# A two-layer attention kernel on one core: loops written out with constant waits, and part of the second layer's vector work given to GpSimd

## The chip, the cores and the metric

The kernel runs on 1 core of one Trainium2 chip. The metric is the device time of one execution in microseconds (us). The core has five engines that run side by side and meet at semaphores: TensorE (PE in the profile, with PEld for its weight loads), VectorE (DVE), ScalarE (ACT), GpSimd (POOL), and SyncE (SP), which here only issues DMAs. Before the change three runs took 2165.38, 2171.02 and 2171.84 us, a median of 2171.02 us.

## The reference, cut to what matters

The input is x of 16 batches x 512 tokens x 128 features, float32. Two layers follow each other, and each adds an attention and a feed-forward part to its input:

```
xn = layernorm(x)
x  = x + attn0(xn) + ffn0(xn)       # 16 heads of 8; q, k through low-rank maps and an RMS norm;
                                    # causal; ffn0: sigmoid gate * (square(relu(.)) @ W_v)
xn = layernorm(x)
x  = x + attn1(xn) + ffn1(xn)       # attn1: softmax(q k^T * scale + bias(position)) v, @ w_proj + b_proj
                                    # ffn1: gelu(xn @ W1) @ W2, W1 and W2 composed once from 32 low-rank pairs
```

So the last line of the second layer sums four things for each token: the residual x, the projected attention, the feed-forward output and b_proj. This sum is one place that the change touches.

## The kernel before, in words

**Bodies and slots.** Each layer is a software pipeline over the 16 batches. One step of it is a "body" (class `Body`). Body n does the scores and the exponentials of batch n, and beside them the preparation for later batches (n+1, n+2) and the closing work of batch n-1. A body has 4 units u (4 heads each) of 16 slots, 64 slots in all. In a slot TensorE computes one 128x512 tile of transposed scores (`scores_t`, L584), which ScalarE exponentiates (L848), and one tile of scores for the row maxima (`scores_max`, L601), which VectorE reduces (L1079 in the first layer, L1084 in the second, there two tiles in one instruction). Four tiles of the second kind fit in PSUM, so TensorE can be at most some three tiles ahead of VectorE (`wait(pe, s["red_done"], ...)`); two tiles of the first kind fit, so it waits for ScalarE's exponential before last (`exp_done`). Every four slots come eight matmuls of probabilities times values (L569).

**The other work.** Everything else is hung on slots by two tables written by hand, `WORK_USES` (uses of the one PSUM bank `work`: the slot at which TensorE fills it, how much later it is taken out, and the batch offset) and `OTHER_WORK`. Each engine walks the slots in order and does what is due on it; each engine's queue runs in that order. In the second layer these matter here:
- `QT` (slot 39) and `KT` (slot 44): queries and keys of batch n+2 are split into three bf16 parts. ScalarE makes the first part, VectorE the remainder (`leave_rest`, L1050), ScalarE the second part (L835), VectorE the third (`third_part`, L1054, three slots after the work bank was taken out first). In the first layer the third part is made on GpSimd (L1126).
- `PR` (slot 30): the projection of batch n-1. VectorE adds the PSUM result and the residual `x_res` (L1038), then the feed-forward output `ffn` (L1041), then the bias `bproj` (L1043), all into `x_new`. These two later additions count up the semaphore `post`.
- `STORE` (slot 32): GpSimd waits for `post` and writes `x_new` with four indirect DMAs (L1139).
- GpSimd multiplies the probabilities next to the diagonal by `near_bias`, once every four slots (L1197), 16 times a body. In the first layer it masks instead (L1183).
- `H0` to `H3` (slots 3, 9, 15, 24): the hidden tiles of the feed-forward part, each with two VectorE instructions (L1060 one slot later, L1066 three slots later). Both read two tensors from SBUF. At the start of each unit VectorE also writes the maxima as two bf16 parts (L963, L965).
- SyncE loads `x_res` at slot 0 (after `post` of the batch before) and `x_tile`, moves the bf16 parts to DRAM and back into `stacks` (L433), and the maxima from `mT` (L448).

**Loops.** Bodies 0 and 1 of a layer are written out, then a loop runs 5 times over two bodies (2 to 11), and bodies from 12 on are written out again: `run_first_layer` (the loop is at L221) and `run_second_layer` (L240). Between the layers `run_both_layers` lets the last bodies of the first layer and the first of the second alternate. In the loop the wait values depend on the loop register, so an engine computes each in a register first (`Body.count`, L250, returns `self.i * (2 * per) + fixed`). `wait_apart` (L253 to L260) puts such a wait in an instruction of its own with an increment of `passed` behind it. All five engines jump back at the loop's end.

## Time and profile before

| | us |
|---|---|
| median of 3 runs | 2171.02 |
| profiled execution | 2168.74 |
| its span, first to last instruction | 2166.6 |
| TensorE busy, share of the span | 1775.1 (82%) |
| VectorE busy | 1610.4 (74%) |
| ScalarE busy | 1338.4 (62%) |
| GpSimd busy | 800.3 (37%) |

The first layer takes roughly the time up to 980 us, the change-over up to 1200 us, the second layer the rest. No engine is busy all the time, so the shares alone do not say what an edit is worth. Since body follows body, the distance from an instruction in one body to the same instruction in the next is the price of a body, and what an engine waits for inside one body tells what sets it. [...]

### The profile page before, as it was taken

To read this page: it belongs to the slowest core of one execution; us is meant where nothing else is said; L and a number is where in the kernel's file an instruction comes from. 1 tells how busy PE (TensorE), PEld (TensorE's weight loads), DVE (VectorE), ACT (ScalarE), POOL (GpSimd) and SP (SyncE) were. 2 spreads that over 40 slices of the span, in tenths; PEclk is the share of its full clock that TensorE was granted. 3 is DMA by queue.
4 is the path that set the end of the run, shared out by engine and by line. 5 is a ranking of instruction groups with operands and counts; after the bars stand their busy time and mean duration, and the time that the engine had idled before them with its cause. 6 is when DMAs were issued, how large, how long until landed. Compare 5 with 4: busy or idle time off the path is not lost.

```text
span 2166.6 us, 41630 instructions
## 1 busy us (share of the span) xinstructions
PE 1775.1 (82%) x12618; PEld 722.7 (33%) x12618; DVE 1610.4 (74%) x2911; ACT 1338.4 (62%) x2518; POOL 800.3 (37%) x824
## 2 busy tenths in 40 slices
PE   5888877778887888878678888888888888888885
PEld 2543333333333333333222332323323333323221
DVE  4367777766677667766378888888898888888881
ACT  1246666655666556655347677777677776777764
POOL 3114443433344334443213344334444344343343
PEclk9769899988999889987669999999999999999998
DMA  7222221221222222220421122221212221222200
GB/s 234 42 45 60 60 56 47 60 61 46 55 52 53 61 55 60 60 55 16 78 45 43 37 60 46 50 56 40 46 44 59 49 50 34 59 45 53 52 11 15
DMA packets 133134, 116.46 MB, mean 54 GB/s; under 512 B 16856, under 2 KB 125664, under 8 KB 132960
## 3 DMA queue, kind: packets, MB, share of 16 engines
q1 hardware_dynamic: 126272, 100.64, 20.1%
q0 software_dynamic: 4096, 8.40, 1.4%
q10 hardware_dynamic: 2592, 5.24, 0.7%
q8 instruction: 93, 1.52, 0.3%
q14 instruction: 81, 0.66, 0.1%
HBM read 79.63 MB, written 33.55 MB: 52 GB/s over the span
## 4 chain that ended last, share of the span: by engine, by line
PE 43%; DVE 21%; issue 16%; ACT 8%; POOL 5%; DMA 3%; SPq 2%; DVEq 1%; ACTq 0%; POOLq 0%
PE pv_acc L569 12%; PE scores_transposed L584 10%; DVE maxs L1084 8%; ACT probs L848 4%; PE work L697 3%; DVE maxs L1079 3%; PE scores_for_max L601 3%; PE work L647 3%; DMA stacks<-parts_scratch 2%; PE work L669 2%; POOL probs L1183 2%; PE work L706 2%; PE work L619 2%; SPq L433 1%; POOL x_between_layers L1139 1%
## 5 line engine op out<-in xcount | busy, mean ns | idle before, releaser
L848 ACT ACTIVATE probs<-scores_transposed 128x512 f32<-128x512 f32 x1664 | 948.0, 600 | 442.6 <-PE scores_transposed L584 437.4
L601 PE MATMUL scores_for_max<-stacks 60*128 60x512 bf16 (+3 forms) x2048 | 659.9, 363 | 102.9 <-DVE maxs L1084 49.4
L584 PE MATMUL scores_transposed<-stacks 62*128 62x512 bf16 (+3 forms) x2048 | 641.6, 360 | 101.7 <-ACT probs L848 86.6
L1084 DVE TENSOR_REDUCE maxs<-scores_for_max 128x2 f32<-128x1024 f32 x512 | 610.9, 1219 | 110.6 <-PE scores_for_max L601 109.3
L1079 DVE TENSOR_REDUCE maxs<-scores_for_max 128x1 f32<-128x512 f32 (+3 forms) x1024 | 446.3, 483 | 253.6 <-PE scores_for_max L606 252.4
L1197 POOL TENSOR_TENSOR probs<-probs,near_bias 128x512 f32<-128x512 f32 x256 | 336.1, 1315 | 638.5 <-ACT probs L848 638.1
L569 PE MATMUL pv_acc<-probs,vals 128*32 128x512 f32 (+3 forms) x4096 | 495.6, 558 | 74.5 <-POOL probs L1183 48.5
L584 PEld LDWEIGHTS scores_transposed<-stacks 62*128 62x128 bf16 x2048 | 162.0, 95 | 755.6 <-ACT probs L848 483.0
L1183 POOL TENSOR_SCALAR_AFFINE_SELECT probs<-probs 128x512 f32<-128x512 f32 x256 | 158.4, 638 | 309.2 <-ACT probs L848 309.1
L601 PEld LDWEIGHTS scores_for_max<-stacks 60*128 60x128 bf16 x2048 | 175.9, 95 | 150.2 <-DVE maxs L1084 78.8
L604 PE MATMUL scores_for_max<-causal_halves,ident_halves 64*128 64x128 bf16 x1024 | 224.6, 233 | 0.0
L606 PE MATMUL scores_for_max<-causal_halves,ident_halves 64*128 64x64 bf16 x1024 | 197.6, 199 | 0.0
L569 PEld LDWEIGHTS pv_acc<-probs,vals 128*32 128x32 f32 x4096 | 83.9, 111 | 210.8 <-issue 127.2
L606 PEld LDWEIGHTS scores_for_max<-causal_halves,ident_halves 64*128 64x128 bf16 x1024 | 107.0, 105 | 55.8 <-issue 15.1
L604 PEld LDWEIGHTS scores_for_max<-causal_halves,ident_halves 64*128 64x128 bf16 x1024 | 98.2, 100 | 0.5
L619 PE MATMUL work<-ident,accS 128*128 128x128 f32 x512 | 93.5, 310 | 5.6 <-ACT mT L763 2.5
L647 PE MATMUL work<-wcat,xnT 128*128 128x512 f32 x128 | 84.6, 747 | 2.6 <-ACT big L784 0.9
L784 ACT ACTIVATE big<-work 128x512 f32<-128x512 f32 x64 | 38.4, 600 | 77.8 <-PE work L647 77.8
L1148 POOL TENSOR_TENSOR rstd<-mv,minus_half 128x4 f32<-128x4 f32 x32 | 33.3, 1039 | 142.1 <-DVE mv L990 142.1
L855 ACT ACTIVATE accS<-pv_acc 128x512 f32<-128x512 f32 x128 | 78.0, 609 | 3.6 <-PE pv_acc L569 3.6
L669 PE MATMUL work<-xnT,w 128*128 128x512 f32 x128 | 76.8, 684 | 2.3 <-DVE att L977 0.8
L1139 POOL DMA_INDIRECT out_dram<-x_new,slots_now x64 | 62.7, 980 | 36.3 <-issue 14.8
(126 smaller groups left out, 1895.9 us busy)
## 6 DMA issues: line engine op xcount, KB each, us to landing
stacks<-parts_scratch SPq DMA_DIRECT2D x768, 64.0 KB
parts_scratch<-parts SPq DMA_DIRECT2D x64, 384.0 KB, 3.0
x_tile<-in_L_attn_x_dram SPq DMA_DIRECT2D x16, 256.0 KB, 2.8
probs<-in_fc_B_dram ACTq DMA_DIRECT2D x1, 4096.0 KB, 19.3
stage_a<-in_fc_A_T_dram SPq DMA_DIRECT2D x1, 4096.0 KB, 16.9
stacks<-mT SPq DMA_DIRECT2D x256, 4.0 KB
x_res<-in_L_attn_x_dram SPq DMA_DIRECT2D x16, 256.0 KB, 3.3
x_tile<-x_between_layers SPq DMA_DIRECT2D x16, 256.0 KB, 2.8
```

The costliest lines, as they stand in the source:

```text
L569: last = mm(acc[32 * j:32 * j + 32, q0:T], vals[:, B.parity(off), kt, G * pu + j, :], probs[:, row, column:column + width], start=(kt == 0 ...
L584: last = mm(st[:, number % 2, column:column + T - q0], ks[p][rows, h, P * kt:P * kt + P], qs[p][rows, h, q0:T], start=True, stop=True)
L601: last = mm(s1[:, i % 4, 0:k1], qs[p][rows, h, P * qt:P * qt + P], ks[p][rows, h, 0:k1], start=True, stop=(layer == 1))
L604: mm(s1[:, i % 4, P * qt:k1], ident_halves[half, 0, :], causal_halves[half, 0, :], start=False, stop=False)
L606: last = mm(s1[:, i % 4, P * qt + HALF:k1], ident_halves[half, 1, :], causal_halves[half, 1, HALF:P], start=False, stop=True)
L619: last = tr(work[:, P * qt:P * qt + P], accS[:, P * qt:P * qt + P], ident[:])
L647: mm(work[:], xnT[:, B.parity(2), 1 + P * t:1 + P * t + P], wcat[:].rearrange("p a n -> p (a n)"), start=True, stop=True).then_inc(full, 1)
L848: fn(probs[:, row, :], st[:, number % 2, :], ACT.Exp, scale=SCALE).then_inc(s["exp_done"], 1)
L1079: v.reduce_max(maxs[:, su % 2, column:column + 1], s1[:, m % 4, 0:P * (qt + 1)], AX_X).then_inc(s["red_done"], 1)
L1084: v.reduce_max(maxs[:, su % 2, :].rearrange("p (e x) -> p e x", e=E)[:, :, column], s1[:, m % 4 - 1:m % 4 + 1, :], AX_X).then_inc(s["red_d ...
L1183: g.affine_select(out=diag, in_=diag, compare_op=ALU.is_ge, fill=0.0, base=0, pattern=[[0, G], [1, P]], channel_multiplier=-1).then_inc(s[ ...
L1197: g.tensor_tensor(diag, diag, near_bias[:, kt, :].unsqueeze(1).broadcast_to([P, G, P]), ALU.mult).then_inc(s["emul_pool"], 1)
```

## The change

Four edits, for all of which the diff is short:
1. Both loops go. Bodies 2 to 11 of each layer are written out like the others, so every wait value is a constant and there is no jump inside a layer.
2. In the second layer GpSimd adds `ffn` and `bproj` to `x_res` at slot 22 (`BESIDE`, semaphore `beside_done`), before the projection. VectorE's addition at `PR` then gives the finished `x_new` in one instruction; `post` is used in the first layer only.
3. In the second layer, too, GpSimd makes the third bf16 parts.
4. Waits follow: the store waits until `PR` was taken out of PSUM, SyncE's load of `x_res` for the same of the body before, and ScalarE's write of `ffn` for `beside_done`.

```
-    1: {"LN": (4, 2), "NORM": (16, 2), "STORE": (32, -1)},
+    1: {"LN": (4, 2), "NORM": (16, 2), "BESIDE": (22, -1), "STORE": (32, -1)},
...
-    with eng.Fori(0, PAIRS) as i:
-        for n in (STEADY, STEADY + 1):
-            run(body(Body(0, n, i)))
-    for n in range(STEADY + 2 * PAIRS, LAST - 1):
+    for n in range(STEADY, LAST - 1):
         run(body(Body(0, n)))
...
                     if u == 0 and B.has(-1):
-                        wait_apart(sp, s["post"], B.count(2, 0, -1), passed)
+                        if layer == 0:
+                            wait(sp, s["post"], B.count(2, 0, -1))
+                        elif B.has(-2):
+                            sp.wait_ge(s["work_taken"], Body(1, B.number - 1).use("PR") + 1)
...
                             if B.has(-1):
-                                act.wait_ge(s["post"], B.count(2, 2, -1))
+                                act.wait_ge(s["beside_done"], B.count(2, 2, -1))
...
-                        if layer == 1 and B.out(name, slot, 3):
-                            third_part(side)
...
                             filled("PR")
-                            dve.wait_ge(s["res_loaded"], B.count(16, 16, -1))
+                            dve.wait_ge(s["beside_done"], B.count(2, 2, -1))
                             wait(dve, s["x_stored"], B.count(16 * NT, 0, -1))
                             v.tensor_tensor(x_new[:].rearrange("p t d -> p (t d)"), work[:],
                                             x_res[:].rearrange("p t d -> p (t d)"), ALU.add).then_inc(taken, 1)
-                            taken_out("PR")
-                            link(v.tensor_tensor(x_new[:], x_new[:], ffn[:, B.parity(-1)], ALU.add),
-                                 "post", 2, 1, -1)
-                            v.tensor_tensor(x_new[:], x_new[:], bproj[:].unsqueeze(1).broadcast_to([P, NT, D]),
-                                            ALU.add).then_inc(s["post"], 1)
...
-                    wait_apart(pool, s["post"], B.count(2, 2, -1), passed)
+                    if layer == 0:
+                        pool.wait_ge(s["post"], B.count(2, 2, -1))
+                    else:
+                        pool.wait_ge(s["work_taken"], B.use("PR") + 1)
...
+                    else:
+                        if B.due("BESIDE", slot):
+                            pool.wait_ge(s["res_loaded"], B.count(16, 16, -1))
+                            g.tensor_tensor(x_res[:], x_res[:], ffn[:, B.parity(-1)], ALU.add
+                                            ).then_inc(s["beside_done"], 1)
+                            pool.wait_ge(s["beside_done"], B.count(2, 1, -1))
+                            g.tensor_tensor(x_res[:], x_res[:], bproj[:].unsqueeze(1).broadcast_to([P, NT, D]),
+                                            ALU.add).then_inc(s["beside_done"], 1)
+                    for side, name in enumerate(("QT", "KT")):
+                        if B.out(name, slot, 3):
+                            third_part(side)
```

What moves is shown at three places of a written-out body of the second layer. First VectorE's queue at `PR` (slot 30), before; a row names the line, the operation, its tiles and in brackets the semaphores that it waits for (`s1_ready`: a tile of scores is there):

```order
L1084 TENSOR_REDUCE maxs<-scores_for_max 128x2 [waits s1_ready_1]
L1038 TENSOR_TENSOR x_new<-work,x_res 128x512 [waits x_stored_1,res_loaded_1,work_full_1]
L1041 TENSOR_TENSOR x_new<-x_new,ffn 128x512 [waits work_taken_1]
L1043 TENSOR_TENSOR x_new<-x_new,bproj 128x512 [waits post_1]
L1084 TENSOR_REDUCE maxs<-scores_for_max 128x2 [waits s1_ready_1]
L963 TENSOR_SCALAR msp<-maxs 128x16 [waits red_done_1]
```

The same place of the same engine's queue now:

```order
L1051 SCALAR_TENSOR_TENSOR big<-fc,fd 128x512 [waits tanh_done_1]
L1069 TENSOR_REDUCE maxs<-scores_for_max 128x2 [waits s1_ready_1]
L1033 TENSOR_TENSOR x_new<-work,x_res 128x512 [waits x_stored_1,beside_done_1,work_full_1]
L1069 TENSOR_REDUCE maxs<-scores_for_max 128x2 [waits s1_ready_1]
L960 TENSOR_SCALAR msp<-maxs 128x16 [waits red_done_1]
```

Two additions between two reductions are gone, and the one that is left waits for GpSimd (`beside_done_1`) in place of the DMA.

Second, VectorE's queue in unit 2, around the first third part, before:

```order
L1084 TENSOR_REDUCE maxs<-scores_for_max 128x2 [waits s1_ready_1] x2
L1050 TENSOR_TENSOR rest<-work,parts 128x512 [waits part0_done_1,work_full_1]
L1084 TENSOR_REDUCE maxs<-scores_for_max 128x2 [waits s1_ready_1]
L1054 TENSOR_TENSOR parts<-rest,parts 128x512 [waits part1_done_1]
L1084 TENSOR_REDUCE maxs<-scores_for_max 128x2 [waits s1_ready_1] x2
```

And the same unit on the same engine now:

```order
L974 TENSOR_TENSOR att<-work,rsum 128x4x32 [waits rec_1]
L1069 TENSOR_REDUCE maxs<-scores_for_max 128x2 [waits s1_ready_1] x2
L1040 TENSOR_TENSOR rest<-work,parts 128x512 [waits part0_done_1,work_full_1]
L1069 TENSOR_REDUCE maxs<-scores_for_max 128x2 [waits s1_ready_1] x3
L1040 TENSOR_TENSOR rest<-work,parts 128x512 [waits part0_done_1,work_full_1]
```

The third part has left the row of reductions.

Third, GpSimd's queue of one body, from `LN` on, before; `probs<-probs,near_bias` is the multiplication of every four slots:

```order
L1148 TENSOR_TENSOR rstd<-mv,minus_half 128x4 [waits ln_1]
L1197 TENSOR_TENSOR probs<-probs,near_bias 128x4x128 [waits exp_done_1] x7
L1134 TENSOR_TENSOR slots_now<-slots_now,a_batch 128x4 [waits x_stored_1]
L1139 DMA out_dram<-x_new,slots_now 8192x128 [waits post_1,slots_moved_1]
L1139 DMA out_dram<-x_new,slots_now 8192x128 x3
L1197 TENSOR_TENSOR probs<-probs,near_bias 128x4x128 [waits exp_done_1] x9
```

The same stretch of GpSimd's queue now:

```order
L1136 TENSOR_TENSOR rstd<-mv,minus_half 128x4 [waits ln_1]
L1193 TENSOR_TENSOR probs<-probs,near_bias 128x4x128 [waits exp_done_1] x4
L1160 TENSOR_TENSOR x_res<-x_res,ffn 128x512 [waits res_loaded_1]
L1163 TENSOR_TENSOR x_res<-x_res,bproj 128x512 [waits beside_done_1]
L1193 TENSOR_TENSOR probs<-probs,near_bias 128x4x128 [waits exp_done_1] x3
L1119 TENSOR_TENSOR slots_now<-slots_now,a_batch 128x4 [waits x_stored_1]
L1127 DMA out_dram<-x_new,slots_now 8192x128 [waits work_taken_1,slots_moved_1]
L1127 DMA out_dram<-x_new,slots_now 8192x128 x3
L1193 TENSOR_TENSOR probs<-probs,near_bias 128x4x128 [waits exp_done_1] x2
L1111 TENSOR_TENSOR parts<-rest,parts 128x512 [waits part1_done_1]
L1193 TENSOR_TENSOR probs<-probs,near_bias 128x4x128 [waits exp_done_1] x2
L1111 TENSOR_TENSOR parts<-rest,parts 128x512 [waits part1_done_1]
```

Four instructions have come into GpSimd's queue: two additions behind the multiplication of slot 20, and two third parts, the first behind the multiplication of slot 40, the second behind that of slot 48.

## Rows read from the trace of the kernel before

**Rows 1.** Windows of the first layer: four bodies with a jump back; five without

```profile
core 0: us, PE busy (x) PEld busy (x) DVE busy (x) ACT busy (x) POOL busy (x), PEclk, DMA share, GB/s
...
sum 244.20, PE 195.57 PEld 90.54 DVE 170.61 ACT 142.44 POOL 93.02; mean PE 48.89 PEld 22.64 DVE 42.65 ACT 35.61 POOL 23.25
...
sum 287.94, PE 232.21 PEld 109.24 DVE 213.70 ACT 178.42 POOL 116.10; mean PE 46.44 PEld 21.85 DVE 42.74 ACT 35.68 POOL 23.22
```

**Rows 2.** Windows of the first layer: two bodies before the loop's steady part, two behind it

```profile
159.49:275.62 116.13, 96.85 (x886) 44.90 (x882) 83.50 (x208) 72.02 (x132) 46.39 (x57) 0.89 0.25 56
...
807.76:920.45 112.69, 92.88 (x869) 43.20 (x868) 84.83 (x209) 71.19 (x131) 46.53 (x58) 0.92 0.25 58
```

**Rows 3.** TensorE's queue at the jumps back: the first layer's, then the second's

```profile
L221 PEldq COMPARE_BRANCH  x5: 76/3717/4063, 351.1 to 826.4; - x5
L240 PEldq COMPARE_BRANCH  x5: 76/208/240, 1366.9 to 1895.5; - x5
```

**Rows 4.** Timeline, TensorE behind a jump, then the same place without one

```profile
355.31 1.35 PE L569 MATMUL pv_acc<-probs,vals 128*32 128x512 f32 x8 [3.81 <-issue]
...
412.20 1.07 PE L569 MATMUL pv_acc<-probs,vals 128*32 128x512 f32 x8 [0.79 <-ACT accS L855]
```

**Rows 5.** Instruction queues (packets, MB, share): first layer's loop; all that the second's has

```profile
q8 instruction: 44, 0.72, 0.6%
...
q14 instruction: 20, 0.16, 0.1%
```

**Rows 6.** Windows of the second layer: nine bodies of the loop, two mostly written out

```profile
1266.72:1861.69 594.97, 521.99 (x3098) 186.38 (x3096) 515.84 (x685) 429.39 (x828) 235.93 (x198) 0.98 0.21 49
1861.69:1992.70 131.01, 112.83 (x690) 38.44 (x688) 113.09 (x153) 95.27 (x184) 52.39 (x44) 0.99 0.20 49
```

**Rows 7.** Waits in eight bodies of the second layer's loop, 1266.72:1795.37 (us in total, times, longest)

```profile
PE scores_transposed L584 <- ACT probs L848: 31.0, 74, 1.0
PE scores_for_max L601 <- DVE maxs L1084: 25.7, 26, 1.9
```

**Rows 8.** Third part by shape in those eight bodies; bias addition by source (min/median/max ns)

```profile
L1054 DVE TENSOR_TENSOR parts<-rest,parts 128x512 bf16<-128x512 f32 x16 | 26.9, 1679 | 0.7
...
L1043 DVE TENSOR_TENSOR x_new<-x_new,bproj x16: 691/1643/1647, 1202.1 to 2154.5; 128x512 f32<-128x512 f32 x16
```

**Rows 9.** Timeline of one loop body: VectorE, GpSimd and TensorE at both moved places

```profile
1399.90 0.69 DVE L1041 TENSOR_TENSOR x_new<-x_new,ffn 128x512 f32<-128x512 f32 x1
1400.62 1.64 DVE L1043 TENSOR_TENSOR x_new<-x_new,bproj 128x512 f32<-128x512 f32 x1
...
1399.99 1.73 POOL L1197 TENSOR_TENSOR probs<-probs,near_bias 128x512 f32<-128x512 f32 x1 [2.45 <-ACT probs L848]
...
1403.46 0.39 PE L601 MATMUL scores_for_max<-stacks 60*128 60x512 bf16 x1 [1.23 <-DVE maxs L1084]
...
1411.85 3.62 DVE L1054 TENSOR_TENSOR parts<-rest,parts 128x512 bf16<-128x512 f32 x1
...
1412.41 2.50 POOL L1197 TENSOR_TENSOR probs<-probs,near_bias 128x512 f32<-128x512 f32 x2
...
1416.67 0.47 PE L601 MATMUL scores_for_max<-stacks 60*128 60x512 bf16 x2 [1.93 <-DVE maxs L1084]
```

**Rows 10.** Windows of two loop bodies: with the 3.62 us row, without it

```profile
1399.17:1465.43 66.26, 57.80 (x346) 20.64 (x344) 57.96 (x77) 47.81 (x92) 26.19 (x22) 0.97 0.21 48
...
1531.31:1597.22 65.91, 58.75 (x346) 20.95 (x344) 55.87 (x77) 47.61 (x92) 26.23 (x22) 0.97 0.20 48
```

**Rows 11.** GpSimd's instructions of the kinds added: third part, addition (min/median/max ns)

```profile
L1126 POOL TENSOR_TENSOR parts<-rest,parts x32: 1152/1153/2471, 48.2 to 936.5; 128x512 bf16<-128x512 f32 x32
...
L1157 POOL TENSOR_TENSOR x_new<-x_res,att x16: 1268/1274/1297, 199.0 to 1062.6; 128x512 f32<-128x512 f32 x16
```

**Rows 12.** Timeline, slots 20 and 30 of one loop body, GpSimd and VectorE

```profile
1457.85 1.27 POOL L1197 TENSOR_TENSOR probs<-probs,near_bias 128x512 f32<-128x512 f32 x1 [1.38 <-ACT probs L848]
...
1465.43 0.69 DVE L1038 TENSOR_TENSOR x_new<-work,x_res 128x512 f32<-128x512 f32 x1
```

More of the change, by code:

```diff
@@ L239, in run_second_layer @@
         run(body(Body(1, n)))
-    with eng.Fori(0, PAIRS) as i:
-        for n in (STEADY, STEADY + 1):
-            run(body(Body(1, n, i)))
-    for n in range(STEADY + 2 * PAIRS, LAST + 1):
+    for n in range(STEADY, LAST + 1):
         run(body(Body(1, n)))
@@ L371, in build @@
                 "red_done", "msplit", "ln", "xn_done", "mix_done", "rms", "rest_done",
-                "rec", "gelu", "hidden_done",
+                "beside_done", "rec", "gelu", "hidden_done",
                 "part2_done", "post",
@@ L1050, in leave_rest @@
                     v.tensor_tensor(rest[:, side], work[:], parts[:, side, 0, :], ALU.subtract).then_inc(taken, 1)
-                def third_part(side):
-                    dve.wait_ge(s["part1_done"], B.count(2, side + 1, 2))
-                    v.tensor_tensor(parts[:, side, 2, :], rest[:, side], parts[:, side, 1, :],
-                                    ALU.subtract).then_inc(s["part2_done"], 1)
                 def gelu_inner(f):
@@ L1168, in other @@
                             g.tensor_tensor(k, k, big[:, :, 2 * P:3 * P], ALU.add).then_inc(s["k_done"], 1)
-                        for side, name in enumerate(("QT", "KT")):
-                            if B.out(name, slot, 3):
-                                third_part(side)
+                    else:
[9 more added lines that the diff above has]
+                            third_part(side)
                 def mask(off, u, kt):
```

## The prediction

> **What bounds the kernel now.** I read the distances from body to body first, since the pipeline repeats, then what TensorE and VectorE wait for inside a body, then the timeline at the places that the change touches.
>
> In the first layer a body is measured from one reciprocal of the RMS norm (slot 34) to the next. Nine such distances lie within the loop. The four that hold the jump back sum to 244.20 us, 61.05 each; the five without it to 287.94 us, 57.59 each [rows 1]. Written-out bodies before and behind take 116.13 and 112.69 us for two, 57.2 each on average [rows 2]. So the jump costs 3.5 us. Its cause stands in TensorE's queue: the branch takes 3717 ns at the median, and only the last one, which falls through, 76 ns [rows 3]. Behind the jump at 351.1 TensorE lies idle for 3.81 us, where in a body without one it waits 0.79 us at the same instruction [rows 4]. In this loop the queue that loads TensorE's instructions moved 44 packets; in the second layer's loop it does not appear at all, the answer lists only the other engines' 20 [rows 5], and the jump there takes 208 ns at the median [rows 3]. The first loop's pair of bodies is loaded anew each time, the second's is not.
>
> [...]
>
> In the second layer nine loop bodies take 594.97 us, 66.1 each, and the next two distances, mostly written out, 131.01 us, 65.5 each [rows 6]. In a body of 66.1 us TensorE is busy 58.0 us and VectorE 57.3 us (521.99/9 and 515.84/9): both are close to full, and they wait for each other. Over eight bodies TensorE waits 25.7 us for VectorE's reductions, 3.2 a body, and 31.0 us for ScalarE's exponentials, 3.9 a body [rows 7]. Two places make most of the first sum [rows 9]. At the projection VectorE does three additions between two reductions, the last of 1.64 us, and TensorE is idle 1.23 us until the next reduction has freed a tile. In unit 2 the third part takes 3.62 us, while GpSimd runs two multiplications back to back, and TensorE is idle 1.93 us. The same kinds of instruction take 0.69 us when nothing is beside them (691 ns is the least for the bias addition) [rows 8]: the rest is waiting for GpSimd.
>
> **The change part by part.**
>
> *First loop written out.* The jumps: 4 x 3.46 us (61.05 less 57.59) = 13.8 us. From below, 4 x 3.02 us (3.81 less 0.79, rows 4) = 12.1 us. The rest of the loop's cost, register arithmetic in front of each wait: 57.59 less 57.2 = 0.4 a body, 10 bodies, 4 us. It lies between 0 and 12 us, because the last two written-out bodies take 56.35 and the first two 58.07 [rows 2]. I take 18 us for the layer, bounds 10 and 26. What is late next at the old jump is ScalarE's copy of the accumulator, the 0.79 us already subtracted.
>
> *Second loop written out.* 66.1 less 65.5 = 0.6 us a body; I take 0.5 for ten bodies, as part of it can overlap the next term: 5 us, bounds 0 and 8. TensorE must now load its instructions here as well; the written-out bodies in the 65.5 us do so already.
>
> *VectorE's two additions at `PR`.* Removed: 0.69 + 1.64 = 2.3 us of VectorE a body [rows 9]. TensorE was idle 1.23 us behind them, so at most about that much is gained at once; I take 1.2.
>
> *The third parts.* Removed from VectorE: 2 x 1.68 us a body on average (1679 ns, rows 8). TensorE was idle 1.93 us in a body with the 3.62 us row. But bodies without it are not shorter by that: 65.91 against 66.26 us at the same mean clock, 0.97 [rows 10]. A mean of 0.97 means that each had its low-level stretch, and in the second the third part fell behind GpSimd's two multiplications in time. I read this as TensorE being late there for another reason, the low clock behind the stall at `PR`, which hid the difference. With both stalls gone neither delay should remain. I take 1.8 us a body for unit 2 and its clock, which with the 1.2 makes 3.0.
>
> Together 3.0 a body is a little under the 3.2 that TensorE waits for VectorE [rows 7]. Lower bound 1.0: both stalls go and TensorE meets ScalarE's exponentials earlier in place of VectorE. Upper bound 4.3: TensorE's own work and its waits for ScalarE, 58.0 + 3.9 = 61.9 us, leave no more of the 66.1. It holds in the 14 bodies that have all this work: 42 us, bounds 14 and 60. In the last body the two additions stand on the path: 0.69 + 0.69 = 1.4 us.
>
> *GpSimd's side.* Third parts cost it 1.15 us each, additions 1.27 [rows 11]: 4.9 us a body on top of 26.2 busy of 66.1 [rows 6], so 31 us, and it is idle half the time. The order on its queue decides. Slot 22: the multiplication of slot 20 ends at 1459.1, two additions end at about 1461.7, the projection's addition starts at 1465.43 [rows 12], so `beside_done` is 3.7 us early. (The addition with the broadcast bias has no row on GpSimd; between 1.15 and 2.5 us, its fastest and slowest two-input rows of this size, I take 1.27.) Behind these additions wait the multiplications of slots 24 and later, whose probabilities TensorE wants a unit (some 16 us) later. Third parts: GpSimd reaches them behind a multiplication that waits for the exponential of slot 43 or 51, so ScalarE's second part (slots 41 and 47) is always there; the DMA that takes the parts stands on SyncE's queue behind a wait for slot 54. `x_res` is loaded at slot 0, and needed at 22 in place of 30. None of this costs anything as long as GpSimd does not fall some ten slots behind.
>
> *Contention.* The rows that were held are gone from VectorE. But VectorE keeps eight gelu instructions and four bf16 splits of the maxima a body with two SBUF inputs, and GpSimd has four more instructions to meet them. The additions of slot 22 run up to VectorE's slot 25 with H3's first gelu instruction. A meeting costs between nothing and the 2.9 us of the 3.62 us row; two short ones a body are in my 3.0.
>
> [...]
>
> **The sum.** 18 + 5 + 42 + 1.4 = 66 us. The profiled execution took 2168.74 us (span 2166.6 and 2.1 around), which gives 2102 us. The median of the runs is 2171.02, 2.3 more; against it the forecast is 2104 us.
>
> **The rivals.**
> 1. *The second layer hardly moves.* TensorE takes up the freed time in waits for ScalarE or in the low clock, and gains 1.0 a body: 18 + 5 + 14 + 1.4 = 38 us, 2133 us. For it: rows 10, where 2.9 us less on VectorE gave 0.35 us. Against: that body still had the other stall.
> 2. *TensorE's own work becomes the bound.* All waits for VectorE go, 4.3 a body, and the first layer gives its upper 26: 26 + 8 + 60 + 1.4 = 95 us, 2076 us. For it: VectorE falls to about 51.6 us of work (57.3 less 5.7) against TensorE's 58. Against: VectorE's load is uneven, and unit 1 alone has H3, the normalisation and `PR`.
> 3. *Slower: loading instructions stalls TensorE in the second layer.* Its loop loads nothing now. A body of it has 346 + 344 matmuls and weight loads [rows 10], one of the first layer some 884 (886 + 882 for two, rows 2), and nine of those moved 44 packets: that is 3.8 packets a body, 38 for ten. If each stalled TensorE like a jump, 3.0 us, that is 114 us; less the 66 gained, 2219 us. It decides from 1.7 us a packet (66/38). Against it: the bodies behind each loop already run so and are the faster ones [rows 2, 6]. The same price would come from GpSimd holding VectorE three times a body.
> 4. *The change does not do what it says.* The last addition waits for GpSimd where it waited for a DMA; were `beside_done` late, the stall at `PR` would stay. It needs GpSimd 3.7 us later than read, and takes the 1.2 a body away, 17 us: 2121 us.
>
> **How the numbers follow.** Forecast, 2090 to 2120: 0.58. Rival 1: 0.17. Rival 2: 0.16. Rival 3: 0.04. Rival 4: 0.05. The likeliest time is 2104 us. The range reaches into both neighbours, 2072 to 2138. Within 0.3% (6.5 us, about what a measurement of this kernel can tell from no change) is left only by a partial rival 3: 0.03; slower 0.04; faster 0.93.
>
> **What the changed profile would show.** No branch rows in TensorE's queue and no idle time over 1.5 us in front of L569 at the places of the jumps; about 57 us a body in the first layer. In the second, bodies of 62.6 us (66.1 less 3.5); TensorE's waits for reductions down from 3.2 to below 1 us a body, its waits for exponentials about as before; VectorE near 51.6 us a body; the third parts on GpSimd at 1.15 us; a low clock less often in unit 2. The queue q8 appears in the second layer. I am wrong if bodies of the second layer stay above 65 us, if the gelu rows (L1060, L1066) grow to several us beside GpSimd, or if idle time by "issue" stands in front of TensorE's instructions every few us.

## The result and the profile after

The changed kernel takes 2084.22 us (median of 4 runs, 2083.3 to 2087.44), the kernel before 2169.42 us beside it. The ratio is 0.9612, with a 95% interval of 0.9592 to 0.9631. So it is 85 us faster where I had forecast 66 us (2104 us). The time lies in the whole range of 2072 to 2138 us, but outside the forecast's own 2090 to 2120, on the side of rival 2 (2076 us). The profiled execution took 2087.44 us with a span of 2085.7 us.

First, part 1 of the page of the changed kernel (busy time, share of the span, instructions):

```profile
PE 1712.9 (82%) x12618; PEld 692.7 (33%) x12618; DVE 1541.2 (74%) x2847; ACT 1333.7 (64%) x2518; POOL 870.5 (42%) x888
```

VectorE has 64 instructions fewer and GpSimd 64 more, four a batch, as the diff says.

Next, windows of before: the ten loop bodies of the first layer, and twelve bodies of the second from the first `x_new` addition on. The columns are those of rows 1; PEclk is TensorE's granted clock as a share of full speed. The clock records behind it hold two values in these traces, 1 and 0.5, here called full and half clock.

```profile
275.62:864.02 588.40, 474.59 (x4341) 221.64 (x4340) 425.94 (x1040) 356.43 (x651) 232.38 (x290) 0.91 0.23 56
1200.66:1992.70 792.04, 693.06 (x4130) 245.04 (x4128) 684.18 (x913) 572.33 (x1105) 314.34 (x263) 0.98 0.21 49
```

The same two stretches of the changed kernel:

```profile
275.88:836.59 560.71, 455.99 (x4341) 212.84 (x4341) 429.13 (x1040) 355.75 (x651) 233.17 (x290) 0.95 0.24 58
1173.75:1923.05 749.30, 658.45 (x4130) 223.79 (x4128) 623.11 (x865) 568.80 (x1105) 365.77 (x311) 1.00 0.22 52
```

The first stretch gives 27.7 us (I had 18, and 26 as the upper bound), the second 42.7. Up to the first stretch nothing changes (275.6 and 275.9), and between the two neither (336.6 and 337.2). The rest, from 1992.70 and 1923.05 to the end of the span, falls from 173.9 to 162.7, 11.2 us. That adds up to the 80.9 us between the spans. A body of the second layer takes 62.4 us (749.30/12), where I had 62.6 and rows 6 show 66.1 and 65.5. TensorE's mean clock over the twelve bodies is 1.00, with no record of half clock, where before it is 0.98, with nine stretches of 3.4 us at 0.5. How far can one profiled execution be trusted? The twelve bodies take 749.0 to 749.4 us in all eight traces that share this code of the second layer. The ten bodies of the first layer are not so steady: a second trace of the changed kernel (further down) has 568.80 us in place of 560.71. Over more traces the gain holds: three with this loop take 592.1 us on average, six without it 563.7.

TensorE's waits in eight bodies of the second layer, 1236.17:1735.80, which answer to rows 7 (us in total, times, longest):

```profile
PE scores_transposed L581 <- ACT probs L845: 37.2, 98, 0.6
...
PE scores_for_max L598 <- DVE maxs L1069: 3.5, 8, 0.5
```

The wait for VectorE's reductions went from 25.7 to 3.5 us, that for the exponentials only from 31.0 to 37.2. So the freed time was not eaten by ScalarE, and rival 1 is out. Rival 2 came half true: nearly all of the wait for VectorE went, and the first layer went past its bound, but a body of the second layer got 3.7 us shorter and not 5.1 (the rival's 4.3 and 0.8). At the projection one addition now stands between two reductions, and GpSimd's third part begins without hindering VectorE (timeline of the changed kernel, first VectorE, then GpSimd; compare rows 9):

```profile
1298.59 0.68 DVE L1033 TENSOR_TENSOR x_new<-work,x_res 128x512 f32<-128x512 f32 x1
1299.19 1.21 DVE L1069 TENSOR_REDUCE maxs<-scores_for_max 128x2 f32<-128x1024 f32 x1
...
1309.99 2.51 POOL L1193 TENSOR_TENSOR probs<-probs,near_bias 128x512 f32<-128x512 f32 x2
1312.44 1.16 POOL L1111 TENSOR_TENSOR parts<-rest,parts 128x512 bf16<-128x512 f32 x1
```

The bias addition, which had no row on GpSimd, by its source line (min/median/max ns); then the instruction queues in the same eight bodies:

```profile
L1163 POOL TENSOR_TENSOR x_res<-x_res,bproj x16: 1273/1281/1289, 1168.8 to 2067.4; 128x512 f32<-128x512 f32 x16
```

```profile
q8 instruction: 22, 0.36, 0.3%
q14 instruction: 20, 0.16, 0.1%
```

The addition with a broadcast input takes 1281 ns at the median, the plain one 1274 [rows 11]. The queue q8, absent from the old loop [rows 5], now moves 22 packets, 2.8 a body (I had 3.8). The twelve bodies all take 62.4 to 62.6 us, so no stall shows at them.

### The profile page after: what moved, and what is told of

The parts are those of the page before. It is cut to its first block, busy times and chain, and to the rows that moved or that the text cites. A ratio compares the mean times of both kernels' runs of the same rounds, so it can differ in the third digit from the quotient of the medians.

```text
span 2085.7 us, 34983 instructions
## 1 busy us (share of the span) xinstructions
PE 1712.9 (82%) x12618; PEld 692.7 (33%) x12618; DVE 1541.2 (74%) x2847; ACT 1333.7 (64%) x2518; POOL 870.5 (42%) x888
## 4 chain that ended last, share of the span: by engine, by line
PE 45%; DVE 23%; ACT 14%; issue 9%; DMA 4%; SPq 3%; POOL 2%; DVEq 0%; POOLq 0%; ACTq 0%
PE pv_acc L566 12%; PE scores_transposed L581 10%; ACT probs L845 7%; DVE maxs L1069 6%; DVE maxs L1064 5%; DMA stacks<-parts_scratch 4%; PE work L694 4%; PE scores_for_max L598 3%; PE work L644 2%; SPq L427 2%; PE work L666 2%; DVE xn L991 2%; PE work L703 2%; DVE msp L962 1%; PE work L616 1%
## 5 line engine op out<-in xcount | busy, mean ns | idle before, releaser
L581 PE MATMUL scores_transposed<-stacks 62*128 62x512 bf16 (+3 forms) x2048 | 631.8, 354 | 122.1 <-ACT probs L845 97.3
L598 PE MATMUL scores_for_max<-stacks 60*128 60x512 bf16 (+3 forms) x2048 | 651.8, 359 | 72.3 <-DVE maxs L1064 33.6
L1193 POOL TENSOR_TENSOR probs<-probs,near_bias 128x512 f32<-128x512 f32 x256 | 329.7, 1291 | 511.3 <-ACT probs L845 510.9
L566 PE MATMUL pv_acc<-probs,vals 128*32 128x512 f32 (+3 forms) x4096 | 480.0, 542 | 61.9 <-issue 33.9
L603 PEld LDWEIGHTS scores_for_max<-causal_halves,ident_halves 64*128 64x128 bf16 x1024 | 105.4, 103 | 54.8 <-issue 12.1
L1111 POOL TENSOR_TENSOR parts<-rest,parts 128x512 bf16<-128x512 f32 x64 | 75.3, 1177 | 96.8 <-ACT parts L832 96.8
L616 PE MATMUL work<-ident,accS 128*128 128x128 f32 x512 | 86.1, 292 | 6.3 <-ACT mT L760 3.3
```

Of the source, the lines that this page charges most:

```text
L566: last = mm(acc[32 * j:32 * j + 32, q0:T], vals[:, B.parity(off), kt, G * pu + j, :], probs[:, row, column:column + width], start=(kt == 0 ...
L581: last = mm(st[:, number % 2, column:column + T - q0], ks[p][rows, h, P * kt:P * kt + P], qs[p][rows, h, q0:T], start=True, stop=True)
L598: last = mm(s1[:, i % 4, 0:k1], qs[p][rows, h, P * qt:P * qt + P], ks[p][rows, h, 0:k1], start=True, stop=(layer == 1))
L603: last = mm(s1[:, i % 4, P * qt + HALF:k1], ident_halves[half, 1, :], causal_halves[half, 1, HALF:P], start=False, stop=True)
L1193: g.tensor_tensor(diag, diag, near_bias[:, kt, :].unsqueeze(1).broadcast_to([P, G, P]), ALU.mult).then_inc(s["emul_pool"], 1)
```

## The experiments

All were compared with the kernel before on the same chip. The chips differ by some microseconds, so I compare ratios, and the windows of the profiles.

**Loops written out, nothing moved.** The kernel before with only this edit, in both layers:

```
-    with eng.Fori(0, PAIRS) as i:
-        for n in (STEADY, STEADY + 1):
-            run(body(Body(1, n, i)))
-    for n in range(STEADY + 2 * PAIRS, LAST + 1):
+    for n in range(STEADY, LAST + 1):
```

> Both loops written out, nothing moved to GpSimd. Theory (the gains add up, the first layer gave 27.7 us and not my 18): 28 us from the first layer and 5 from the second, about 2136 us against 2169, ratio 0.985. Rival (the first layer's extra 10 us over my 18 came with the moves or with a lucky clock): 23 us, about 2146 us, ratio 0.989. The second layer's bodies at 65.5 us by both.

Measured: 2135.35 us, ratio 0.9842 (0.9785 to 0.9899). Windows of the two stretches:

```profile
275.77:837.91 562.14, 463.75 (x4341) 216.69 (x4341) 422.34 (x1040) 355.73 (x651) 233.26 (x290) 0.93 0.24 58
1177.72:1957.05 779.33, 667.53 (x4130) 224.81 (x4128) 682.71 (x914) 572.67 (x1105) 313.74 (x263) 1.00 0.21 50
```

The first layer's gain is all here: 26.3 us of the 27.7. The second layer surprised: 12.7 us, where I had 5. Its bodies take 64.9 us on average (779.33/12), not the 65.5 of the bodies behind the old loop. The total came out as expected.

**Moves only.** The changed kernel with both loops back.

> Both loops kept, the sum and the third parts on GpSimd. Theory (gains add up): 52.5 us less 5 for the second loop, 47 us, about 2122 us, ratio 0.978; bodies of the second layer near 62.9 us, first layer as before at 58.8. Rival (the moves need constant waits to pay, since register arithmetic stands in TensorE's and VectorE's queues): 35 us or less, bodies of 63.7 us or more, ratio above 0.984.

Measured: 2120.57 us, ratio 0.9772 (0.9716 to 0.9828).

```profile
273.87:869.45 595.58, 481.28 (x4341) 225.06 (x4340) 426.73 (x1041) 356.94 (x651) 232.20 (x290) 0.90 0.24 55
1202.86:1957.41 754.55, 677.14 (x4130) 243.98 (x4128) 625.98 (x866) 569.77 (x1105) 365.33 (x311) 1.00 0.22 51
```

The moves give 37.5 us in twelve bodies with the loop (792.04 to 754.55), 30.0 without (779.33 to 749.30). Constant waits give 5.2 us on top of the moves (754.55 to 749.30), 12.7 without them. So 7.5 us go with whichever edit comes first. Either edit also takes the low clock away: the mean over the twelve bodies is 0.98 before and 1.00 with one of the two edits. In time at half clock that is 30.7 us before, in nine stretches, 3.4 with the loops written out, in the one stretch below, and none with the moves:

```profile
1183.10:1186.52 3.42, 3.42 (x16) 0.97 (x13) 1.59 (x3) 1.31 (x3) 2.33 (x2) 0.50 0.11 31
```

How much of the 7.5 us comes from this is not shown. The rival, that the moves need constant waits, falls. As times the two edits add up: 33.9 us and 48.7 us alone, on one chip, against 85.2 and 79.0 together, on two others.

**The first layer's loop alone back, plain and with a fetch hint.** The second kernel differs from the first by one option of the loop, which puts one more instruction at the head of each pass, a hint to fetch the loop's start ahead of the jump:

```
-    for n in range(STEADY, LAST - 1):
+    with eng.bass.Fori(0, PAIRS, engines=OrderedEngineSet([eng.engine]), hint_back_edge=True) as i:
+        for n in (STEADY, STEADY + 1):
+            run(body(Body(0, n, i)))
+    for n in range(STEADY + 2 * PAIRS, LAST - 1):
```

> The changed kernel with the first layer's loop put back. Theory: the first layer loses all of its 27.7 us, about 2112 us, ratio 0.974; four idle stretches of 3.4 to 4 us on TensorE behind the jumps. Rival (lucky clock): 18 us or less, 2102 us.

> As the one before, but each pass of the first layer's loop begins with a hint to fetch the loop's start ahead of the jump back. Theory (the jump costs 13.8 us through the load of instructions, register arithmetic the other 14): TensorE's branches well under 1 us, no idle time of 3.4 us and more behind them, and about 14 us less than with the plain loop, 2098 us. Rival 1 (registers cost nothing, the stall and the low clock behind it are all): 2085 us. Rival 2 (the hint does not help, or TensorE stalls for another reason): 2112 us, branches still 3.6 us.

Measured: 2118.62 us plain, ratio 0.977 (0.9713 to 0.9827), and 2115.9 us with the hint, 0.9759 (0.9704 to 0.9814). As times the two can't be told apart; the traces can. Plain: the window of the ten bodies, then TensorE's branches, then the timeline of TensorE behind the first jump:

```profile
278.82:871.21 592.39, 474.70 (x4341) 222.67 (x4340) 426.39 (x1041) 357.08 (x651) 232.31 (x290) 0.91 0.25 55
```

```profile
L221 PEldq COMPARE_BRANCH  x5: 76/3843/4097, 355.9 to 832.3; - x5
```

```profile
360.12 1.94 PE L569 MATMUL pv_acc<-probs,vals 128*32 128x512 f32 x8 [3.81 <-issue]
```

With the hint, the same three:

```profile
277.35:854.57 577.22, 473.65 (x4341) 221.73 (x4340) 419.66 (x1040) 356.84 (x651) 232.34 (x290) 0.90 0.23 56
```

```profile
L222 PEldq COMPARE_BRANCH  x5: 80/405/436, 354.2 to 817.1; - x5
```

```profile
355.34 1.07 PE L570 MATMUL pv_acc<-probs,vals 128*32 128x512 f32 x8 [0.79 <-ACT accS L856]
```

The hint takes the branch from 3.8 to 0.4 us and the idle time behind it from 3.81 to the 0.79 us of a body without a jump [rows 4]. In these two executions the ten bodies lose 15.2 us; my term for four jumps was 13.8. From there to the written-out loop are another 16.5 us (577.22 to 560.71), for which I had 4. The plain loop put back costs 31.7 us in these bodies, and 2118.62 us is 7 more than expected. But with the hint the whole kernel gained only 2.7 us, and its time is the one that I had given for a hint that does not help (2112 us), not the 2098 us of the theory. In the profiled executions 10.3 of the 15.2 us were lost again between the loop and the second layer (342.2 us against 331.9), and from the start of the ten bodies to the first `x_new` addition of the second layer TensorE stood at half clock for 249 of 919.4 us (mean clock 0.86), against 225 of 924.3 us without the hint (0.88). The other executions point the same way: the mean granted clock was 0.913 to 0.918 in the four with the hint and 0.918 to 0.923 in the four without. So with the hint the stall is gone, and most of its time came back while the mean clock was lower; what brought the clock down is not shown.

**One of the two moves at a time.** First the third parts back on VectorE (the sum on GpSimd), then the sum back, with `BESIDE` gone from GpSimd's program (the third parts on GpSimd); loops written out in both:

```
+                        if layer == 1 and B.out(name, slot, 3):
+                            third_part(side)
```

```
-                        if B.due("BESIDE", slot):
```

> The changed kernel with the third bf16 parts back on VectorE (the sum stays on GpSimd). Bodies of the second layer were 64.8 us written out without the moves and 62.4 with both. Theory (each stall is worth itself): half of the 2.4 us is lost, bodies near 63.6 us, 17 us more in all, about 2101 us. Rival 1 (VectorE has room once the sum is gone, the third parts cost nothing): 62.4 to 62.7 us, 2085 us. Rival 2 (the second stall takes the place of the first): 64.5 us and more, 2114 us.

> The changed kernel with the sum back on VectorE in three additions behind the projection (the third parts stay on GpSimd). Theory (each stall is worth itself): bodies near 63.6 us, and 1.4 us at the end, about 2102 us. Rival 1 (the third parts alone were the stall): 62.7 us and less, 2088 us. Rival 2 (the sum's stall takes all): 64.5 us and more, 2114 us.

Measured: 2100.44 us, ratio 0.9665 (0.961 to 0.972), and 2128.15 us, 0.9812 (0.977 to 0.9854). Twelve bodies of the first, then its third parts in eight of them by shape (busy, mean ns | idle before), then one meeting with GpSimd in the timeline:

```profile
1173.28:1936.49 763.21, 662.45 (x4130) 223.25 (x4128) 658.70 (x889) 572.54 (x1105) 339.13 (x287) 1.00 0.22 51
```

```profile
L1046 DVE TENSOR_TENSOR parts<-rest,parts 128x512 bf16<-128x512 f32 x16 | 29.1, 1816 | 1.1
```

```profile
1311.28 2.51 POOL L1200 TENSOR_TENSOR probs<-probs,near_bias 128x512 f32<-128x512 f32 x2
1311.40 2.95 DVE L1046 TENSOR_TENSOR parts<-rest,parts 128x512 bf16<-128x512 f32 x1
```

Twelve bodies of the second, and one body of it at the full clock:

```profile
1179.19:1951.76 772.57, 671.14 (x4130) 226.34 (x4128) 648.28 (x890) 568.94 (x1105) 340.61 (x287) 0.99 0.21 50
...
1436.97:1500.72 63.75, 55.44 (x346) 18.75 (x344) 53.97 (x76) 47.36 (x93) 28.36 (x24) 1.00 0.22 51
```

The third parts are worth 13.9 us in twelve bodies (763.21 less 749.30), 1.2 each: 63.6 us a body, as expected. (As a time this is less sure: one of the four executions took 2085.13 us, the others some 2101.) The sum is worth 23.3, 1.9 each. In its bodies at full clock it is 1.3 (63.75 against 62.42); the other six lie near 65.1 and hold a stretch of 3.4 us at half clock, each right behind TensorE's wait of 1.2 us at `PR`. It is worth more at the end of the program too: 176.3 us from the last of these bodies on, against 162.7, with 34 us at half clock against 13.5 (mean clock 0.90 and 0.96). So 2128 us is more than any of the three expectations: the theory had left out the low clock and most of the end. (The profiled execution was also 9.1 us longer in the ten bodies of the first layer, where the code is the same.)

**A loop of four bodies in the second layer.** Two passes, so one jump; all wait values scaled to four bodies:

```
+    with eng.Fori(0, 2) as i:
+        for n in range(STEADY, STEADY + 4):
...
-        return fixed if self.i is None else self.i * (2 * per) + fixed
+        return fixed if self.i is None else self.i * (self.bodies * per) + fixed
```

> The changed kernel with a loop in the second layer again, but over four bodies (two passes, one jump back), about 3300 instructions on TensorE where the old pair had about 1700. Theory (a jump stalls TensorE when the loop does not fit what it holds): the one jump takes 3 to 4 us in TensorE's queue, an idle stretch of some 3 us behind it, the instruction queue q8 runs all the time, and with 0.5 us a body for the registers about 7 us in all, 2091 us. Rival (the first layer's stall has to do with that layer's code, not with size): the jump takes 0.2 us as in the old loop of two bodies, 2088 us.

Measured: 2101.54 us, ratio 0.9701 (0.9653 to 0.9748). The body with the jump and three windows at it; then TensorE's branches (min/median/max ns); then the matmul behind the jump:

```profile
1430.50:1500.52 70.02, 60.59 (x346) 21.04 (x344) 51.56 (x73) 47.42 (x93) 30.43 (x26) 0.93 0.20 47
...
1461.00:1465.00 4.00, 0.47 (x2) 0.17 (x2) 2.12 (x2) 2.22 (x5) 1.26 (x1) 1.00 0.04 8
1465.00:1469.00 4.00, 3.27 (x14) 1.03 (x14) 0.35 (x2) 0.60 (x1) 0.00 (x0) 0.53 0.04 8
1469.00:1473.00 4.00, 3.74 (x10) 0.81 (x8) 3.51 (x8) 1.68 (x3) 1.21 (x1) 0.50 0.00 0
```

```profile
L238 PEldq COMPARE_BRANCH  x2: 79/2015/3951, 1461.5 to 1720.3; - x2
```

```profile
1465.73 1.93 PE L574 MATMUL pv_acc<-probs,vals 128*32 128x512 f32 x8 [3.95 <-issue]
```

In the kernel with the moves alone the same bodies were looped over as a pair, and TensorE's branches there were:

```profile
L240 PEldq COMPARE_BRANCH  x5: 76/208/240, 1359.5 to 1863.3; - x5
```

The same code that jumps in 0.2 us as a pair stalls TensorE for 3.95 us as a group of four: here size decides, not the code. From one jump to the next the traces hold 1656 instructions of TensorE for this pair (1376 of them matmuls and weight loads), 2066 for the first layer's pair of the kernel before, which stalls, and 3282 for four bodies. So the 0.2 us stand at 1656 instructions and the stalls at 2066 and 3282; that a loop stalls when it does not fit what TensorE holds is my theory for it, and no run shows what TensorE holds. Of the 2066, 1734 are matmuls and weight loads and 314 register arithmetic. And the one jump costs 7.1 us (70.02 against 62.9 of its neighbours), more than the idle stretch itself, and TensorE then runs at half clock for about 10 us (0.53 and 0.50 in the windows above, 0.93 over the body). The twelve bodies take 760.2 us in all, 10.9 more than written out, where I had 7: the 7.1 of the jump, and 0.5 a body in the others of the loop.

**Going on in the first layer.** With the loops gone, these were TensorE's longest waits in the ten bodies of the changed kernel, 275.88:836.59:

```profile
PE pv_acc L566 <- issue: 23.9, 10, 2.4
PE scores_for_max L598 <- DVE maxs L1064: 21.7, 24, 1.3
PE work L621 <- DVE att L974: 15.2, 10, 1.5
```

The first stands once a body in front of the matmuls of probabilities at slot 28 (not 22 to 24, as the expectation below has it). My theory for it: GpSimd made each mask only one group of four slots ahead and had the sum and four store DMAs in front of it. The second trace of the changed kernel bears this out, as it names the mask: its row for the same wait, then one meeting, the last store's issue and the masks on GpSimd and the matmuls behind them:

```profile
PE pv_acc L566 <- POOL probs L1179: 25.8, 20, 2.4
```

```profile
320.11 0.95 POOL L1127 DMA_INDIRECT x_between_layers<-x_new,slots_now  x1 [0.30 <-issue]
321.07 1.23 POOL L1179 TENSOR_SCALAR_AFFINE_SELECT probs<-probs 128x512 f32<-128x512 f32 x2
321.78 0.59 PE L566 MATMUL pv_acc<-probs,vals 128*32 128x128 f32 x8 [2.36 <-POOL probs L1179]
```

Five kernels ran. The first makes a unit's masks together; the second is the changed kernel with only the loads of the stacks moved up; the third has both; the fourth also puts `MT0` of the first layer from slot 4 to 5; the changed kernel itself ran beside the last two.

```
-                            if kt < NT - 1 and B.has(mo):
-                                mask(mo, mu_, kt + 1)
+                            if kt == 0 and B.has(mo):
+                                for later in range(1, NT):
+                                    mask(mo, mu_, later)
...
-                    if u < 2 and B.has(1):
-                        load_stack(u)
+                    if u == 0 and B.has(1):
+                        for side in range(2):
+                            load_stack(side)
```

> The changed kernel with the first layer's masks of a unit made together at its first slot (they were made one group of four slots ahead of their use), so that GpSimd's sum and store at slots 21 and 22 no longer stand in front of the mask that TensorE needs at slot 22 to 24. Theory: TensorE's idle 2.4 us there goes in some 14 bodies, 30 us less, about 2054 us, bodies of the first layer near 53.8 us. Rival (VectorE's reductions or the exponentials take the freed time, or GpSimd's mask now waits for the last exponential and holds back other work): less than 10 us, bodies of 55.3 us and more.

> The changed kernel with both stacks loaded in the first unit, the masks where they were. Masks alone took the ten first-layer bodies from 560.7 to 546.5 us, masks and stacks to 519.3. Theory (the loads matter only once the masks no longer stall TensorE, since TensorE waited 0.9 us in ten bodies for them in the changed kernel): within 5 us of the changed kernel, ratio 0.960 to 0.965. Rival (the loads cost time in a way the waits do not show): 20 us less, ratio 0.952 and below.

> Masks early as before, and SyncE loads both stacks of the next batch in the first unit, not one in each of the first two. With the masks early TensorE waited 14.1 us in ten bodies for these loads (9 times, at most 2.8). Theory (the loads come too late because they start too late): that wait goes, 14 us less than with the masks alone, first-layer bodies near 53.2 us, ratio about 0.951. Rival (the loads are bound by the queues, or starting them early delays the maxima's small DMA behind them on SyncE): no gain or a loss, ratio 0.958 or more.

> As the one before, and the first layer's first transposition of the maxima one slot later (5 in place of 4). TensorE waited 1.5 us a body there for VectorE to take out what stood in the one work bank. Theory: most of it goes, 1.0 us a body, 14 us, ratio about 0.945. Rival (the wait moves to the next use of the bank, at slot 6): no change against the one before.

> The changed kernel itself, to stand beside the next two on one chip: 2084 us, ratio 0.961, within some 5 us.

Measured:

| kernel | us | ratio (95%) |
|---|---|---|
| masks early | 2074.18 | 0.9581 (0.9531 to 0.9632) |
| stacks early only | 2082.0 | 0.9588 (0.9546 to 0.9631) |
| both | 2016.95 | 0.9291 (0.9243 to 0.9339) |
| both, `MT0` at 5 | 2015.27 | 0.9297 (0.9233 to 0.9361) |
| changed kernel again | 2093.31 | 0.9648 (0.9609 to 0.9686) |

The windows of the ten first-layer bodies, one of each kernel: masks early,

```profile
269.17:815.72 546.55, 465.49 (x4344) 217.82 (x4340) 413.40 (x1041) 356.94 (x650) 233.32 (x290) 0.92 0.24 60
```

stacks early only,

```profile
263.81:823.71 559.90, 455.56 (x4341) 214.01 (x4341) 429.27 (x1041) 355.42 (x651) 233.19 (x290) 0.95 0.22 58
```

both,

```profile
258.97:778.29 519.32, 442.24 (x4341) 209.38 (x4341) 414.56 (x1041) 355.23 (x651) 233.07 (x290) 0.96 0.25 63
```

and the changed kernel again:

```profile
274.62:843.42 568.80, 469.64 (x4341) 217.79 (x4341) 427.56 (x1040) 355.39 (x651) 232.71 (x290) 0.92 0.24 57
```

Masks early give about half of what I expected (546.6, 54.7 a body, not 53.8), because the next wait stood behind the first: TensorE then waited for the loads of the stacks (masks early, same kind of row):

```profile
PE scores_for_max L598 <- DMA stacks<-parts_scratch: 14.1, 9, 2.8
```

The loads alone give nothing in these bodies that can be told from zero (559.9 against 560.7 and 568.8), but the bodies ahead of them end some 11 us earlier (at 263.81, where the changed kernel's two traces have 275.88 and 274.62). Together with the masks they give 41 to 50 us in these ten bodies, where I expected 28, and in the whole kernel 77 us by the ratios on one chip (0.9291 against 0.9648). Of the 72 us between the two profiled executions 49.5 lie in the ten bodies, 15.7 ahead of them and 6.0 between them and the second layer. So the masks alone gave less than expected (2074 us against 2054), and the pair more (ratio 0.9291 against 0.951). The two waits that went, 23.9 and 14.1 us, come to 38 us of the ten bodies' gain; TensorE's mean clock is also higher, 0.96 against 0.95 and 0.92. The best kernel here is 7% faster than before. `MT0` at 5 took its own wait away, but the one for the reductions doubled, and the time did not change; that theory fell. The changed kernel itself took 2093 us here, 9 more than the first time, so between chips a difference of that size means little. The two waits in the ten bodies, first with `MT0` at 4, then at 5:

```profile
PE work L622 <- DVE att L975: 15.2, 10, 1.5
PE scores_for_max L599 <- DVE maxs L1065: 12.5, 15, 1.3
```

```profile
PE scores_for_max L599 <- DVE maxs L1065: 24.1, 26, 1.3
...
PE work L622 <- DVE att L975: 1.7, 10, 0.2
```

## Why the prediction was right or wrong

**Direction and mechanism: right.** TensorE and VectorE bounded the second layer together, and TensorE's idle time behind the two places of rows 9 was the price. In written-out bodies at the full clock each stall was worth 1.2 to 1.3 us (62.4 with none, 63.6 with the third parts' alone, 63.75 with the sum's). For the sum I had 1.2. For the third part I had 1.8, "with its clock". In the loop, which is where I had read the 3.0 a body, the two moves gave 3.1 (37.5/12); in written-out bodies 2.5 (30.0/12). Taken in this order, moves first, both terms of the second layer came out: 37.5 us in twelve bodies (I had 36), then 5.2 for the loop (I had 5). One slip: 66.1 less 61.9 is 4.2, so rival 2's bound was 59 us and not 60.

**The jump: the stall right, its price in the whole not shown.** I forecast 13.8 us, and the hint took 15.2 us out of the ten bodies in one execution each. The whole kernel gained 2.7 us. The four-body loop shows that the stall goes with the size of the loop (0.2 us at 1656 instructions, 3.95 us at 3282). The one jump there also shows that my 3.0 us of idle time is only part of the price.

**"Register arithmetic in front of each wait ... 0.4 a body": mis-sized.** The spans differ by 80.9 us, 14.5 more than my sum of 66.4; 9.7 of them lie here, in the first layer, and 3.8 at the end of the program. I measured this step by four written-out bodies of the old trace, 57.2 us on average, two of them at 58.07. In six traces with the first layer as in the changed kernel, two of them of that kernel, the ten bodies take 557.0 to 569.8 us, 56.4 a body on average; with register values and the hint they take 57.7. So the step is worth 1.3 a body (13.5 us in ten), of which one execution can show 0.7 to 2.0, and only one trace has the hint. The four bodies near the ends were no fair sample: the first two ran at a mean clock of 0.89 [rows 2]. Most of the step is not idle time: with the hint TensorE is busy 473.65 us at a mean clock of 0.90, in the changed kernel's two traces 455.99 at 0.95 and 469.64 at 0.92, for the same matmuls. So the step goes with more time at half clock; whether the register instructions bring that about is not shown. In the second layer, with a mean clock of 1.00 in both windows, the kernel with register values has TensorE busy for 18.7 us more (677.14 against 658.45) with instructions of the same mean length (385 ns for both kinds of score tiles, 605 and 604 for the probabilities), and idle for 13.4 us less: the matmuls follow each other less closely.

**"I read this as ... the low clock behind the stall at `PR`": right for these rows.** The body without the 3.62 us row [rows 10] had its low stretch just there. The matmul behind the wait at `PR`, and the low stretch as a window, in the kernel before:

```profile
1535.60 0.39 PE L601 MATMUL scores_for_max<-stacks 60*128 60x512 bf16 x1 [1.24 <-DVE maxs L1084]
```

```profile
1537.00:1540.40 3.40, 3.40 (x18) 0.95 (x10) 1.97 (x5) 1.16 (x4) 2.12 (x3) 0.50 0.09 21
```

All twelve bodies before split in this way. In five the low stretch of 3.4 us began 1.0 to 1.6 us behind the wait at `PR`, and the wait of 1.9 us in unit 2 did not come; in the other seven it came, with a low stretch behind it in four. So the two delays stood in for each other, and the bodies are nearly equally long, 65.9 and 66.1 us on average. What does not hold is that such a wait brings the low clock each time: with the sum's stall alone six bodies of twelve had a low stretch, with the third parts' alone none. With the loops written out and both stalls in place it was one, though TensorE still waited 27.3 us in eight bodies for the reductions (the kernel with only the loops written out):

```profile
PE scores_for_max L595 <- DVE maxs L1078: 27.3, 32, 1.3
```

What decides it stays open.

**The end: too small.** My 3.0 a body held for the two full bodies behind the twelve, and the two additions were to give 1.4 in the last, 7.4 in all; it was 11.2. The two bodies gave 3.4 and 2.8 us. The tail came out: from the last `x_new` addition to the end of the span 13.6 us before (2166.6 less 2153.03), 12.1 after. What I had put at nothing is the body between them, from the last `x_new` addition but one to the last: 38.0 us before, 34.4 after. With the loops written out and the sum still on VectorE it takes 41.8 us with nothing moved and 42.6 with the third parts moved, 19 and 20 of them at half clock (mean clock 0.77 and 0.76), so there the sum costs 7 to 8 us.

**GpSimd: right.** It is busy 30.5 us a body of 62.4 (365.77/12; I had 31), and delays nothing: in the eight bodies TensorE waits for none of its instructions. VectorE is busy 51.9 us a body (I had 51.6). Rival 3 (loading stalls TensorE) and rival 4 (`beside_done` late) did not come: bodies of 62.4 us with q8 at work, and 3.5 us of waits for reductions in eight bodies. The meetings that I had feared hardly show: VectorE's first gelu instruction takes 708 ns on average, where it took 690.

## What to carry to other kernels

In a pipeline whose steps repeat, measure one step from trace to trace by the same instruction, and price a stall by the idle time of the engine it holds, not by the length of the instruction that causes it: 5.7 us taken from VectorE gave 2.5 to 3.1 us. Count the instructions of a loop: with 1656 of TensorE the jump took 0.2 us, with 2066 and 3282 TensorE stood idle for 3.8 to 3.95 us behind it, and behind the one of 3282 came about 10 us at half clock. The fetch hint cut the branch from 3.8 to 0.4 us, but the time followed by only 2.7 us; straight code did better. Bodies at the edge of a loop are a poor measure of straight code in its middle. And when one wait is gone, look for the next behind it before the edit is judged: in the ten bodies, masks and loads were worth 14 to 22 and 1 to 9 us alone, and 41 to 50 together (against the changed kernel's two traces).

## What the runs showed of the hardware that was not expected

- One jump out of a loop of four bodies: 3.95 us without work on TensorE, then about 10 us at half clock, 7.1 us in all. The hint instruction takes 36 ns and cuts the branch from 3.8 to 0.4 us; the whole kernel gained 2.7 us by it.
- TensorE's queue jumped back in 0.2 us with 1656 instructions in the loop, and stalled with 2066 and with 3282.
- VectorE's third part, which has two inputs from SBUF and takes 0.68 us at the least, took 2.95 us across two multiplications on GpSimd that run back to back, so it was not let in between them, as the 3.62 us row [rows 9] across such a pair (that row began 0.6 us before the pair, beside the issue of the last store).
- GpSimd's addition with an input broadcast along a dimension took 1281 ns at the median, the one without 1274 [rows 11].
